# Attention of sixteen small heads: one list of finer steps ordered by due times, and the reciprocal as ln and exp on ScalarE

## What is computed

```python
x, ctx = normalised input, context   16 sequences, 128 queries, 128 keys, 16 heads of 16
q = (x @ Wq + bq).reshape(B, N, 16, 16).transpose(0, 2, 1, 3)
k, v = the same of ctx with Wk, Wv
attn = softmax(einsum('bhnd,bhkd->bhnk', q * 16 ** -0.5, k), axis=-1)
out = einsum('bhnk,bhkd->bhnd', attn, v)
x = x + out.transpose(0, 2, 1, 3).reshape(B, N, 256) @ Wproj + bproj
```

## Time and profile before

| | us |
|---|---|
| median of 3 runs (lowest, highest) | 4432.84 (4424.89, 4438.37) |
| the profiled execution: its time | 4435.27 |
| its span, first to last instruction | 4433.8 |
| TensorE busy, share of the span | 3279.0, 74% |
| VectorE busy | 2479.3, 56% |
| ScalarE busy | 1624.7, 37% |
| GpSimd busy | 1407.1, 32% |
| mean granted TensorE clock | 0.86 of full speed |
| stage 7, start to end in the span | 2936.6 to 3209.9 |
| stage 10 | 3926.2 to 4199.8 |

### The profile page before, as it was taken

How to read it: one execution, slowest core, us unless ns; L and a number is a source line. 1 busy time by engine, 2 the same in 40 slices (tenths; PEclk the granted TensorE clock), 3 DMA queues, 4 the chain that set the end, 5 groups by cost and what they waited for, 6 DMA issues and landing times. The chain is left out here.

```text
span 4433.8 us, 52962 instructions
## 1 busy us (share of the span) xinstructions
PE 3279.0 (74%) x17693; PEld 2111.6 (48%) x17693; DVE 2479.3 (56%) x6511; ACT 1624.7 (37%) x3647; POOL 1407.1 (32%) x1086
## 2 busy tenths in 40 slices
PE   5988887867925677766888888466679666767698
PEld 3666665646612233223566656345456422335555
DVE  6878784364336888885323323535442278855443
ACT  3666654111204544542333334224302144424311
POOL 4666664103452444452212212200010245520010
PEclk7888887888967888888999999679869778989899
DMA  2000000302430000000000000110021200000000
GB/s 89 5 9 6 9 8 9 124 20 82 127 111 39 0 0 0 0 0 14 7 1 1 1 1 1 37 78 1 13 101 29 74 0 1 0 27 1 1 1 20
DMA packets 71034, 116.12 MB, mean 26 GB/s; under 512 B 28689, under 2 KB 58537, under 8 KB 68018
## 3 DMA queue, kind: packets, MB, share of 16 engines
q1 hardware_dynamic: 61170, 86.50, 5.8%
q0 software_dynamic: 9600, 26.23, 2.4%
HBM read 88.58 MB, written 24.12 MB: 25 GB/s over the span
## 5 line engine op out<-in xcount | busy, mean ns | idle before, releaser
L1224 POOL TENSOR_TENSOR L_attn_state<-L_attn_state,L_attn_ccol 128x1024 f32<-128x1024 f32 x192 | 452.3, 2356 | 527.5 <-DVE L_attn_state L1217 526.1
L1217 DVE TENSOR_TENSOR_SCAN L_attn_state<-L_attn_decay,bank 128x1024 f32<-128x1024 f32 x192 | 438.3, 2283 | 41.1 <-ACT L_attn_decay L1194 15.3
L1183 PE MATMUL bank<-L_attn_state,ident 128*128 128x512 f32 x768 | 421.2, 678 | 19.4 <-POOL L_attn_state L1224 19.3
L1177 PE MATMUL bank<-L_attn_parts,L_attn_select 96*128 96x512 bf16 x384 | 137.9, 441 | 256.7 <-DVE bank L1209 241.8
L1194 ACT ACTIVATE L_attn_decay<-L_attn_dt,L_attn_A 128x512 f32<-128x512 f32 x384 | 256.2, 716 | 129.3 <-DVE L_attn_state L1217 116.3
L1103 POOL TENSOR_TENSOR L_xattn_prob<-L_xattn_prob,L_xattn_inv 128x1024 f32<-128x1024 f32 x64 | 121.2, 1895 | 567.2 <-DVE L_xattn_inv L1086 567.2
L1209 DVE TENSOR_TENSOR bank<-L_attn_dtx,bank 128x1024 f32<-128x1024 f32 x192 | 236.0, 1229 | 57.0 <-PE bank L1177 50.7
L1183 PEld LDWEIGHTS bank<-L_attn_state,ident 128*128 128x128 f32 x768 | 164.7, 217 | 185.4 <-issue 129.9
L1177 PEld LDWEIGHTS bank<-L_attn_parts,L_attn_select 96*128 96x128 bf16 x384 | 29.9, 102 | 391.0 <-DVE bank L1209 340.0
L736 ACT ACTIVATE L_xattn_prob<-bank,L_xattn_top 128x128 f32<-128x128 f32 x512 | 135.8, 416 | 195.9 <-DVE L_xattn_top L778 195.9
L1027 ACT ACTIVATE L_xattn_prob<-L_xattn_masked,L_xattn_low 128x256 f32<-128x256 f32 x256 | 127.0, 497 | 209.2 <-DVE L_xattn_low L1081 127.3
(11 more groups left out here) (601 smaller groups left out, 7705.4 us busy)
## 6 DMA issues: line engine op xcount, KB each, us to landing
L_ffn_ew<-in_L_ffn_experts SPq DMA_DIRECT2D x4, 3072.0 KB, 21.2
L_ffn_made<-L_ffn_yout SPq DMA_DIRECT2D x24, 512.0 KB, 3.0
L_ffn_w<-in_L_ffn_w SPq DMA_DIRECT2D x4, 2048.0 KB, 14.6
L_xattn_ctx<-in_ctx_rows SPq DMA_DIRECT2D x3, 2048.0 KB, 8.2
L_ffn_rows<-L_ffn_xh SPq DMA_DIRECT2D x8, 512.0 KB, 2.9
L_ffn_made<-L_ffn_yout SPq DMA_DIRECT2D x12, 256.0 KB, 2.1
L_attn_rows<-in_x SPq DMA_DIRECT2D x16, 128.0 KB, 6.9
turned<-L_attn_rows SPq DMA_DIRECT2D x16, 128.0 KB, 2.3
```

Of the source, the lines that this page charges most:

```text
L1177: pe.matmul(self.spread.bank(2 * N + i)[:, :], self.select[:, NSTATE * i + n, :], parts[:, :], start=True, stop=True).then_inc(*self.sprea ...
L1183: t = pe.matmul(self.y[unit % len(self.y)][m][:, :], self.c.ident[:, :], self.state[N % 3][:, m, :], start=n == 0, stop=n == 15)
L1217: dve.tensor_tensor_scan(flat(self.state[N % 3]), flat(self.decay[N % 2]), flat(self.drive), 0.0, ALU.mult, ALU.add).then_inc(*self.scanne ...
L1224: pool.tensor_tensor(state[:, :, :], state[:, :, :], self.ccol[N % 2][:, :].unsqueeze(1).broadcast_to([P, 2, GT]), ALU.mult).then_inc(*sel ...
```

## The change

Steps are made finer: `soft` is split into `max` (VectorE) and `exp` (ScalarE) per bank, and each fill of `turn`, `q`, `k`, `value` and `flip` is a step of its own, with its emptying as another (`turned`, `qcopy`, `kcopy`, `vcopy`, `flipped`); `mix` is followed by `inverse` and `blend`, `out` by `add`. The order is now made by sorting: `HEADS_BY_UNIT` and `HEADS_BY_GROUP` give each step a due time in units, and `as_due` yields all steps of all units and groups by that time, so that steps of three units lie among each other (unit u's scores are due at u + 0.3, its mix at u + 1.81, its `out` at u + 2.88). The first group's front comes ahead of that list. Where a fill may now come before its old copy would have been read, the copies of q, k and v wait for the last use of the buffer two groups ago. The reciprocal of the row sums on VectorE becomes ln and then exp with scale -1 on ScalarE (`inverse`), and the stage begins by asking for the table set that holds both functions. `Fills.done` and `as_due` gain assertions on the order.

```diff
@@ class Fills @@
+        self.latest = {}
...
-        return self.gone[self.by[n % len(self.by)]].up()
+        e = self.by[n % len(self.by)]
+        assert n > self.latest.get(e, -1)
+        self.latest[e] = n
+        return self.gone[e].up()
@@ new functions @@
+def due_by(table, period, turns):
+
+    for kind, at in table.items():
+        each = at if isinstance(at, tuple) else (at,)
+        yield from ((period * turn + time, kind, len(each) * turn + i) for turn in turns for i, time in enumerate(each))
+
+
+def as_due(due):
+
+    latest = {}
+    for _, kind, n in sorted(due):
+        assert n > latest.get(kind, -1)
+        latest[kind] = n
+        yield kind, n
 
@@ new tables @@
+HEADS_BY_UNIT = {"max": (0.19, 0.33, 0.42, 0.52), "score": 0.3, "exp": (0.34, 0.54, 0.56, 0.92), "flipped": (0.65, 1.03, 1.11, 1.32),
+                 "flip": (0.73, 0.86, 0.94, 1.6), "mix": 1.81, "inverse": 1.83, "blend": 1.88, "out": 2.88, "add": 2.97}
+HEADS_BY_GROUP = {"stats": -4.35, "norm": -3.52, "turned": (-3.3, -2.82, -2.73, -2.15), "turn": (-3.17, -2.99, -2.77, -2.23), "q": (-2.52, -2.06),
+                  "qcopy": (-2.5, -1.71), "kcopy": (-1.69, -1.27), "k": (-1.49, -1.2), "value": (-1.06, -0.38), "vcopy": (-0.94, -0.47)}
@@ many_heads @@
-    topped, inverted = s.flag("topped", 4), s.flag("inverted")
+    topped, logged, inverted, masked = s.flag("topped", 4), s.flag("logged"), s.flag("inverted"), s.flag("masked")
     row = lambda n: X[:, n, :]
 
     def order():
-        def front(g):
-            return [("norm", g), ("stats", g + 1), ("turn", 4 * g), ("turn", 4 * g + 1), ("turn", 4 * g + 2), ("turn", 4 * g + 3),
-                    ("k", 2 * g), ("q", 2 * g), ("k", 2 * g + 1), ("q", 2 * g + 1), ("value", 2 * g), ("value", 2 * g + 1)]
         yield "begin", 0
         yield "stats", 0
-        yield from front(0)
-        ahead = []
-        for u in range(NSEQ + 2):
-            if u < NSEQ:
-                if u % GROUP == 0:
-                    ahead = front(u // GROUP + 1) if u + GROUP < NSEQ else []
-                yield "score", u
-                yield "soft", u
-            if 2 <= u:
-                yield "out", u - 2
-            if 1 <= u <= NSEQ:
-                for j in range(4):
-                    yield "flip", 4 * (u - 1) + j
-                    if j != 1 and ahead:
-                        yield ahead.pop(0)
-                yield "mix", u - 1
-            else:
-                for _ in range(3):
-                    if ahead:
-                        yield ahead.pop(0)
+        yield "norm", 0
+        yield "stats", 1
+        for what, copied, times in (("turn", "turned", 4), ("k", "kcopy", 2), ("q", "qcopy", 2), ("value", "vcopy", 2)):
+            for n in range(times):
+                yield what, n
+                yield copied, n
+        yield from as_due([step for step in chain(due_by(HEADS_BY_UNIT, 1, range(NSEQ)), due_by(HEADS_BY_GROUP, GROUP, range(1, NGROUP))) if step[1:] != ("stats", 1)])
 
...
     def empty_value(engine, copy, n):
         g, half = divmod(n, 2)
         at = side["value", n]
+        if g >= 2:
+            engine.wait_ge(*mix.filled(GROUP * (g - 2) + GROUP - 1))
         engine.wait_ge(*side.filled(at))
         made = side.bank(at)[:, :].rearrange("p (b h r e) -> p b h r e", b=2, r=2, e=hd)
         to = v[g % 2][:, 2 * half:2 * half + 2, :, :].rearrange("p b (h r) e -> p b h r e", r=2)
@@ -715,28 +727,36 @@
 
     def scalar(what, n):
         if what == "begin":
+            act.preload_act_table_set(EXP_AND_LN)
             act.wait_ge(*begun.at(1))
-        elif what == "turn" and n % 2 == 0:
+        elif what == "turned" and n % 2 == 0:
             empty_turn(act, act.copy, n)
-        elif what == "q":
+        elif what == "qcopy":
             g, m = divmod(n, KC)
-            at = side[what, n]
+            at = side["q", n]
+            if g >= 2:
+                act.wait_ge(*score[3].filled(GROUP * (g - 2) + GROUP - 1))
             act.wait_ge(*side.filled(at))
             for parity in range(2):
                 t = act.activation(q[g % 2][parity][:, m, :], side.bank(at)[:, :], ACT.Identity, bias=bq[:, parity, m:m + 1], scale=mask[:, parity:parity + 1])
             t.then_inc(*side.done(at))
-        elif what == "value" and n % 2 == 0:
+        elif what == "vcopy" and n % 2 == 0:
             empty_value(act, act.copy, n)
-        elif what == "soft":
-            for j in range(4):
-                if j == 0 and n >= 2:
-                    act.wait_ge(*flip.filled(4 * (n - 2) + 3))
-                act.wait_ge(*topped.at(n, j))
-                for i in range(4):
-                    t = act.activation(prob[n % 2][j][:, i, :], score[j].bank(n)[:, i * P:(i + 1) * P], ACT.Exp, bias=top[:, j, i:i + 1])
-                t.then_inc(*score[j].done(n))
-        elif what == "flip" and n % 2 == 0:
+        elif what == "exp":
+            u, j = divmod(n, 4)
+            if j == 0 and u >= 2:
+                act.wait_ge(*flip.filled(4 * (u - 2) + 3))
+            act.wait_ge(*topped.at(u, j))
+            for i in range(4):
+                t = act.activation(prob[u % 2][j][:, i, :], score[j].bank(u)[:, i * P:(i + 1) * P], ACT.Exp, bias=top[:, j, i:i + 1])
+            t.then_inc(*score[j].done(u))
+        elif what == "flipped" and n % 2 == 0:
             empty_flip(act, act.copy, n)
+        elif what == "inverse":
+            act.wait_ge(*mix.filled(n))
+            act.activation(inv[:, :, :], mix.bank(n)[:, 2 * P:4 * P].rearrange("p (m k) -> p m k", m=KC), ACT.Ln).then_inc(*logged.up())
+            act.wait_ge(*logged.at(n))
+            act.activation(inv[:, :, :], inv[:, :, :], ACT.Exp, scale=-1.0).then_inc(*inverted.up())
 
     def vector(what, n):
         if what == "begin":
@@ -750,8 +770,8 @@
             for parity in range(2):
                 dve.memset(one[:, parity, parity * hd:(parity + 1) * hd], 1.0)
             t = dve.tensor_scalar(mask[:, :], mask[:, :], hd ** -0.5, None, ALU.mult)
-            t.then_inc(*inverted.up())
-            dve.wait_ge(*inverted.at(0))
+            t.then_inc(*masked.up())
+            dve.wait_ge(*masked.at(0))
             for parity in range(2):
                 t = dve.tensor_scalar(bq[:, parity, :], w["bqk"][:, 0, :], mask[:, parity:parity + 1], None, ALU.mult)
             t.then_inc(*begun.up())
@@ -763,30 +783,30 @@
             if n:
                 dve.wait_ge(*side.filled(side["turn", 4 * n - 3]))
             norm.apply(n, lambda b: row(GROUP * n + b), lambda b: xh[:, b, :])
-        elif what == "turn" and n % 2:
+        elif what == "turned" and n % 2:
             empty_turn(dve, dve.tensor_copy, n)
-        elif what == "k":
+        elif what == "kcopy":
             g, m = divmod(n, KC)
-            at = side[what, n]
+            at = side["k", n]
+            if g >= 2:
+                dve.wait_ge(*score[3].filled(GROUP * (g - 2) + GROUP - 1))
             dve.wait_ge(*side.filled(at))
             dve.tensor_scalar(kT[g % 2][:, m, :], side.bank(at)[:, :], w["bqk"][:, 1, m:m + 1], None, ALU.add).then_inc(*side.done(at))
-        elif what == "value" and n % 2:
+        elif what == "vcopy" and n % 2:
             empty_value(dve, dve.tensor_copy, n)
-        elif what == "soft":
-            for j in range(4):
-                dve.wait_ge(*score[j].filled(n))
-                dve.tensor_reduce(top[:, j, :], score[j].bank(n)[:, :].rearrange("p (i k) -> p i k", i=4), AX.X, ALU.max, negate=True).then_inc(*topped.up())
-        elif what == "flip" and n % 2:
+        elif what == "max":
+            u, j = divmod(n, 4)
+            dve.wait_ge(*score[j].filled(u))
+            dve.tensor_reduce(top[:, j, :], score[j].bank(u)[:, :].rearrange("p (i k) -> p i k", i=4), AX.X, ALU.max, negate=True).then_inc(*topped.up())
+        elif what == "flipped" and n % 2:
             empty_flip(dve, dve.tensor_copy, n)
-        elif what == "mix":
-            dve.wait_ge(*mix.filled(n))
-            dve.reciprocal(inv[:, :, :], mix.bank(n)[:, 2 * P:4 * P].rearrange("p (m k) -> p m k", m=KC)).then_inc(*inverted.up())
+        elif what == "blend":
             if n >= 2:
                 dve.wait_ge(*side.filled(side["out", n - 2]))
-            dve.wait_ge(*inverted.at(n + 1))
+            dve.wait_ge(*inverted.at(n))
             dve.tensor_tensor(oT[n % 2][:, :, :], mix.bank(n)[:, 0:2 * P].rearrange("p (m k) -> p m k", m=KC), inv[:, :, :], ALU.mult).then_inc(*mix.done(n))
-        elif what == "out":
-            at = side[what, n]
+        elif what == "add":
+            at = side["out", n]
             if n % GROUP == 0:
                 dve.wait_ge(*shifted.at(n // GROUP))
             dve.wait_ge(*side.filled(at))
```

## The result

| | us |
|---|---|
| before, median of 4 runs (lowest, highest) | 4432.99 (4424.89, 4438.37) |
| after, median of 4 runs (lowest, highest) | 4290.81 (4280.9, 4295.25) |
| ratio after to before, 95% interval | 0.9679 (0.9667 to 0.9691) |
| forecast | 4298 (4262 to 4375) |

A forecast was written before the change was run, and what follows sets the result against it. No engine is full, so the order of hand-overs between engines was taken as the bound. Gains of 9.7, 28.6 and 30.1 us make 68.4 per stage, 137 for two: 4435.3 - 137 = 4298, range 4262 to 4375.

The forecast's parts named there:

- A plain unit: Unit without projections, stepped through engine by engine: 8.2 us score to score instead of 14.3, scores waiting last for exp 3.
- Units with projections: Groups of four sharing one bank for fills: 42.3 us against 56.6; third unit 12.35, its value fill waiting for the add.
- Units 0 to 3: First group of a stage: 41.0 us against 50.7, with 1.5 for a first unit at the lower clock.
- Unit 12 to the end: End of a stage, three plain units and the drain: 39.7 us against 69.8, gain 30.1.
- The inverse: Ln and exp of 128x256 on ScalarE replacing VectorE's 1.76 us reciprocal: 0.87 us, between bounds of 0.75 and 1.35.
- The start: Beginning of a stage, fills still one by one through one bank: 39.7 us, unchanged.
- The table set: Load at stage start asks for the set already held; at most one load of 1.28 us under the normalisation.
- What would show it: Signs: plain units 8 us, groups' units 8 to 12.5, stages about 205, maxima wait under 35, clock over 0.9 from unit 12.
- the low clock in plain units: Rival 1: clock stays lower in plain units, 10.8 us instead of 8.2; 10 us per stage, 4318; chance 0.12.
- Longer hand-overs: Rival 2: hand-overs between engines 0.1 to 0.2 us longer, 1 to 2 us per unit; 4330 to 4362; chance 0.17.
- the order brings nothing: Rival 3: only the reciprocal leaves the way to the maxima, 1.15 us in each of 32 units; 4395; chance 0.08.
- The tables: Rival 4: ln and exp lie in different table sets, switches give 82 us back; 4380; chance 0.03.

The follow-up runs named there:

- the run with two ln: Changed kernel with the ln done twice, the first time into a spare buffer, in each of 32 units: 0.9699 of the kernel before.
- the order alone: Changed kernel with the reciprocal back on VectorE, placed behind the copy of the turned context: 0.9715 of the kernel before.
- 64 loads: Changed kernel with two table loads on ScalarE (another set, and back) behind each inverse: 0.9859 of the kernel before.

## Why the prediction was right, step by step

The forecast was 4298, measured were 4291. The mechanism was the one described, and most terms of the sum held. Part of the closeness is luck all the same: within the group of four the misses of +0.4, -0.15, +0.05 and -0.3 us cancel. In the traces the two stages gained 145.3 us, where the forecast has 137; the stages between them took 2.3 us more, and the forecast was reckoned from an execution that was 2.4 us over the median.

- *A plain unit, 8.2 us.* Measured 7.8. The last wait was the one named, scores for exp 3. The 0.4 us are mainly the idle time that the walk put before exp 1: TensorE turned the fourth bank 1.1 us after the scores began, so VectorE's copy and max 1 were over by the time exp 0 was.
- *Units with projections, 42.3 us for a group.* Measured 42.3; by unit 10.9, 11.1, 12.4 and 7.9 against 10.5, 11.25, 12.35 and 8.2. The size of the third was right and its reason only half: the value fill waits for the add, as walked, but for some 0.26 us only. The walk had the add behind the inverse; it stands behind TensorE's output projection, so what holds the unit is TensorE's own work, as the run with two ln and the rows above show.
- *Units 0 to 3, 41.0 us.* Measured 38.9; unit 0 took 8.9 where 8.3 and 1.5 for a low clock were added up, and unit 1 was 0.7 us shorter.
- *Unit 12 to the end, 39.7 us.* Measured 39.2: 1.2 us less in three plain units, 0.7 more in the drain (15.8 instead of 15.1).
- *The inverse, 0.87 us.* Measured 0.38 and 0.42 us, 0.74 from the start of the ln to the start of exp 3. That exp 3 starts 0.09 us before the row of the inverse's exp is over was left out.
- *The start, 39.7 us, unchanged.* 40.0 in the first stage and 36.0 in the second, where it was 39.8. A term was missing: 3.8 us, of them 3.6 from a clock that rose two projections earlier (last section). The gains were 70.6 and 74.7 us against 68.4 each.
- *The table set.* The prediction said that the earlier stages' set is held. The trace has one load of 1.283 us at the start of each of the two stages, under the normalisation as the second half of that sentence allowed, so it cost nothing.
- *What would show it.* Score to score as said; the stages 202.7 and 198.9 us for "about 205"; ScalarE's wait for maxima 28.0 us for "under 35"; clock 1.00 from unit 12 on; no load between ln and exp. The add as the last wait in the third unit came too, though it holds less than the walk had it hold. The list was not complete: in the first and second unit of a group a fill of the shared bank waits for the add as well (0.32 us in each), as the walk says and the list of signs does not.

The rivals: the low clock in plain units did not come (1.00). Longer hand-overs did not come: the plain unit took less than the walk's 8.2 us. That the order brings nothing is refuted by the order alone at 0.9715. The tables: no load between ln and exp, and 64 loads cost 77 us, against 82 by the row. The clock at 1.2 GHz all through: the lowest unit of the changed kernel is the first of each stage, at 0.81, and from unit 12 on it is 1.00.

What the 142 us are made of, as far as runs show it: the order alone 126, with 3.6 of the second stage's start in it; the move of the reciprocal to ScalarE 13 to 16, where it brought 35 in the old order. A clock that no longer falls in the plain units is some 10 of the 126, if it is worth there what it was worth in the kernel before with its gap filled, which is an inference. It may not be all that the clock gives: TensorE runs the same 2052 instructions in each stage and is busy 163 and 159 us where it was 180 and 181. How much of that was on the path in the other units no run tells.

## What to carry to other kernels

Where no engine is full, write one steady period of each engine's stream side by side with durations from the trace, and follow the wait that ends last; such a walk named the lengths of units here within 0.4 us, the first two of a stage aside (0.9 and 0.7), and where it had a reason wrong, two chains of nearly the same length ended there. A step in an in-order queue costs what stands behind it: the same reciprocal cost 13 us in one place and 31 to 34 in another, where its due time was 0.03 of a unit earlier. Under the chain that is shortened lies the next: in the plain units here it was 0.2 us below, so ask what will end last before shortening one further.

## What the runs showed that was not expected

- A pair of table loads runs at 1.283 us each with 0.01 us between them and beside them.
- Four matmuls that nobody reads, in a gap of 3.4 us, made the kernel before 10 us faster: the granted clock of the unit rose from 0.76 to 1.00.
- The start of the second stage took 36.0 us where it was 39.8. From the first turning of the context to the first scores it is 22.7 us in all eleven traces (of ten kernels) that ask for the table set at the stage's begin, the old order with ln and exp among them, and 26.3 in the two that don't, the kernel before and the same with its gap filled. TensorE's rows, first of the changed kernel, then of the one with the gap filled:

```profile
3870.90 1.12 PE L623 MATMUL bank<-ident,L_xattn_ctx 128*128 128x128 f32 x4 [0.78 <-DVE L_xattn_xT L706]
...
3874.59 3.48 PE L634 MATMUL bank<-L_xattn_cT,L_xattn_wk 128*128 128x512 f32 x4 [0.78 <-DVE L_xattn_cT L706]
3878.91 1.98 PE L634 MATMUL bank<-L_xattn_cT,L_xattn_wk 128*128 128x512 f32 x4 [0.84 <-DVE L_xattn_kT L794]
```

```profile
3938.96 3.78 PE L624 MATMUL bank<-L_xattn_cT,L_xattn_wk 128*128 128x512 f32 x4 [0.78 <-DVE L_xattn_cT L700]
3943.59 3.78 PE L624 MATMUL bank<-L_xattn_xT,L_xattn_wq 128*128 128x512 f32 x4 [0.85 <-DVE L_xattn_kT L776]
3948.91 3.51 PE L624 MATMUL bank<-L_xattn_cT,L_xattn_wk 128*128 128x512 f32 x4 [1.54 <-ACT L_xattn_q L730]
```

The context's turning is at the low level (1.12 us in both; four such matmuls take 0.63 in the unit shown above). In the first the clock rises within the first projection (3.48 us, then 1.98), in the second within the third (3.78, 3.78, 3.51). The idle times before the first two projections are the same within 0.01 us. As the old order has it too, the order of k and q isn't the cause. The load by itself isn't enough either: the first stage of the changed kernel has the same load, and there the stretch takes 26.6 us, where it took 26.3 before. Whether the load plays a part in the second stage, or something ahead of it, was not tried and stays open.
